# Two-layer GNN kernel: the first batch's sorted groups moved ahead of the first set's sort

## What is computed

```
h = relu(layernorm(x))
agg = segment_sum((h * node_vec1)[src], dst, 12500)      # layer 0: gather, sum by destination
x = x + agg * node_vec1_n2
h = relu(layernorm(x))
m = relu(h[src] + edge_attr_32)                          # layer 1: gather, add the edge's features
x = x + (1 + eps[0]) * h + segment_sum(m, dst, 12500)
```

## Time and profile before

| | us |
|---|---|
| median of three runs | 4798.12 (4794.34 to 4802.32) |
| the profiled execution | 4791.23 |
| its span | 4789.2 |
| busy in it: PE / DVE / ACT / POOL | 3721.2 / 3812.7 / 3261.3 / 3497.5 |

### The profile page before, as it was taken

How to read it: one execution, slowest core, us unless ns; L and a number is a source line. 1 busy time by engine, 2 the same in 40 slices (tenths; PEclk the granted TensorE clock), 3 DMA queues, 4 the chain that set the end, 5 groups by cost and what they waited for, 6 DMA issues and landing times.

```text
span 4789.2 us, 130194 instructions
## 1 busy us (share of the span) xinstructions
PE 3721.2 (78%) x43852; PEld 2888.9 (60%) x43852; DVE 3812.7 (80%) x11454; ACT 3261.3 (68%) x9090; POOL 3497.5 (73%) x3590
## 2 busy tenths in 40 slices
PE   0388888888888888888888899467767777777775
PEld 0266666666666666666666666356666666666664
DVE  9788888888888888888888886767777776777775
ACT  1377777777777777777777777456666766666664
POOL 6757777777777777777777777477777777777774
PEclk9999999999999999999999999778888888888887
DMA  6322222222222222222222221211212221211221
GB/s 111 63 51 54 57 54 54 54 56 54 54 54 56 54 53 54 56 54 53 54 56 54 53 54 44 72 39 54 57 43 54 57 57 54 58 49 48 57 57 26
DMA packets 439702, 262.77 MB, mean 55 GB/s; under 512 B 334660, under 2 KB 423732, under 8 KB 432632
## 3 DMA queue, kind: packets, MB, share of 16 engines
q1 hardware_dynamic: 322488, 187.55, 16.7%
q0 software_dynamic: 110816, 60.69, 6.7%
q10 hardware_dynamic: 5728, 5.82, 0.5%
HBM read 172.96 MB, written 80.85 MB: 53 GB/s over the span
## 4 chain that ended last, share of the span: by engine, by line
PE 32%; POOL 23%; DVE 19%; issue 13%; ACT 10%; DMA 2%; DVEq 1%; ACTq 0%; SPq 0%; POOLq 0%
POOL stage L759 22%; PE candidates L1247 18%; PE plain_ps L1259 7%; DVE arena L1753 7%; ACT message L987 5%; DVE arena L1729 4%; ACT centered L956 2%; PE sorted_agg L1187 2%; PE candidates L1157 1%; ACT arena L880 1%; POOL message L759 1%; PE key_rows L1230 1%; DMA stage<-in_edge_attr 1%; DVE counts L1475 1%; PE key_rows L1139 1%
## 5 line engine op out<-in xcount | busy, mean ns | idle before, releaser
L771 POOL DMA_INDIRECT records<-stage,place_i x1875 | 1879.0, 1002 | 696.2 <-issue 652.0
L759 POOL DMA_INDIRECT stage<-table,src_plain x1250 | 1246.9, 997 | 409.1 <-issue 377.3
L987 ACT ACTIVATE message<-candidates,member_is 128x96 bf16<-128x96 f32 x4560 | 1170.7, 377 | 429.4 <-PE candidates L1247 426.3
L1753 DVE TENSOR_SCALAR arena<-window_iota,dst_rel 128x224 bf16<-128x224 f16 (+1 forms) x4800 | 1091.2, 302 | 37.8
L880 ACT ACTIVATE arena<-key_rows 125x640 f16<-125x640 f16 x1000 | 653.2, 716 | 215.1 <-DVE arena L1729 83.2
L1187 PE MATMUL sorted_agg<-arena 128*96 128x224 bf16 (+1 forms) x5000 | 654.1, 285 | 161.0 <-DVE arena L1753 109.6
L1259 PE MATMUL plain_ps<-summed,message 128*96 128x224 bf16 x4560 | 609.2, 269 | 68.2 <-ACT message L987 68.2
L1187 PEld LDWEIGHTS sorted_agg<-arena 128*96 128x96 bf16 x5000 | 543.7, 137 | 186.1 <-issue 118.6
L1259 PEld LDWEIGHTS plain_ps<-summed,message 128*96 128x96 bf16 x4560 | 490.7, 128 | 269.6 <-ACT message L987 127.4
L1729 DVE TENSOR_SCALAR arena<-arena,row_key 125x1280 bf16<-125x1280 f16 x1000 | 554.7, 555 | 96.5 <-ACT arena L880 64.6
L1139 PE MATMUL key_rows<-ident,record 128*125 128x128 f16 x5000 | 425.8, 235 | 239.2 <-DMA record<-records 96.2
(11 more groups left out here) (228 smaller groups left out, 5139.0 us busy)
## 6 DMA issues: line engine op xcount, KB each, us to landing
record<-records SPq DMA_DIRECT2D x50, 1650.0 KB
stage<-in_edge_attr SPq DMA_DIRECT2D x125, 400.0 KB, 3.2
records<-pad SPq DMA_DIRECT2D x25, 1650.0 KB, 11.9
records<-stage,place_i POOLq DMA_INDIRECT x1875
stage<-table,src_plain POOLq DMA_INDIRECT x1250
message<-table,mid_src POOLq DMA_INDIRECT x288
xs<-in_x SPq DMA_DIRECT2D x8, 390.6 KB
table<-parts ACTq DMA_DIRECT2D x4, 585.9 KB
```

Source lines behind the costliest of these rows:

```text
L759: pool.indirect_dma_start(message[:, k, j, :] if l == 0 else rows[:, k, j, :], None, table0 if l == 0 else table1, bass.IndirectOffsetOnAx ...
L771: pool.indirect_dma_start(records, bass.IndirectOffsetOnAxis(ap=place_i[:, h, e:e + 1], axis=0), stage[:, h, e, :], None).then_inc(scatter ...
L987: last = nc.scalar.activation(direct_message[n % DB][:, m * WIDE:(m + 1) * WIDE], candidates[n % 2][:, m * WIDE:(m + 1) * WIDE], ACT.Copy, ...
L1753: last = nc.vector.tensor_scalar(dst_onehot(g, t), window_iota[:, 0:WA if tile == 0 else WT], dst_rel[:, h, tile:tile + 1], None, ALU.is_e ...
```

## The change

In batch 0 only, all three engines take the ten sorted groups first. DVE sorts the first set and reads the words of batch 0 behind them, right ahead of the wide steps. ACT issues the two DMAs of the trip behind the groups, and the direct keys of the first two wide steps are turned (PE) and copied (ACT) behind them as well.

```diff
@@ ACT, ahead of the layers
                     act.wait_ge(words_out, 32)
                     act.dma_start(set_left, words_rows[0:P, :]).then_inc(set_loaded, 16)
-                    act.wait_ge(set_steps, SET_STEPS)
-                    act.dma_start(ordered_rows[0:P, :], set_left).then_inc(words_out, 16)
-                    act.wait_ge(words_out, 48)
-                    act.dma_start(row_words, ordered_v[:, 0:SET, :]).then_inc(words_loaded, 16)
@@ ACT, step0
-                        if g in (7, 8) and not is_last(b):
+                        if g in (7, 8) and not is_first(b) and not is_last(b):
                             copy_direct_keys(b, g - 7)
...
                     over_main_groups(group)
+                    if is_first(b):
+                        act.wait_ge(set_steps, SET_STEPS)
+                        act.dma_start(ordered_rows[0:P, :], set_left).then_inc(words_out, 16)
+                        act.wait_ge(words_out, 48)
+                        act.dma_start(row_words, ordered_v[:, 0:SET, :]).then_inc(words_loaded, 16)
+                        copy_direct_keys(b, 0)
+                        copy_direct_keys(b, 1)
                     copy_sorted(b, 0)
@@ PE, step0
-                        if g in (7, 8) and not is_last(b):
+                        if g in (7, 8) and not is_first(b) and not is_last(b):
                             turn_direct_keys(b, h, g - 7)
...
                     over_main_groups(group)
+                    if is_first(b):
+                        turn_direct_keys(b, h, 0)
+                        turn_direct_keys(b, h, 1)
@@ DVE, ahead of the layers
-            dve.wait_ge(bounds_ready, 2 * PJ + 1)
-            sort_set(0, range(ROUNDS8))
-            dve.wait_ge(words_loaded, 16)
-            read_words(0, 0, 0)
@@ DVE, step0, behind over_main_groups(group)
                     else:
+                        if is_first(b):
+                            dve.wait_ge(bounds_ready, 2 * PJ + 1)
+                            sort_set(0, range(ROUNDS8))
+                            dve.wait_ge(words_loaded, 16)
+                            read_words(0, 0, 0)
```

## The result

The changed kernel takes 4812.59 us, the median of 18 runs (4806.34 to 4819.23). The kernel before, run beside it on the same chip, takes 4803.85 us, the median of 18 runs (4794.34 to 4813.91). The ratio is 1.0019, with a 95% interval of 1.0012 to 1.0026: some 9 us slower (5.8 to 12.5 us). The forecast was 9.0 us, and 4807 us in all. The measured time lies 5.6 us above that, as the kernel before does too: its median of 18 runs is 5.7 us above the 4798.12 us from which the forecast started. Two executions among the experiments, 7372.95 us of the kernel before and 6088.68 us of the one with all three steps, are far slower than the rest of their kernel and are left out of the ratios.

What follows compares the result with a forecast made beforehand. DVE was taken to set the time up to 304 us, with everything behind hanging on its end of batch 0. 7.2 + 0 + 0 + 1.5 + 0.3 = 9.0 us on 4798.1 gave 4807 us, range 4799 to 4816 us.

Steps and rivals of the forecast that it cites:

- The first hole: Ahead of DVE's first piece: waiting for record, turned and copied keys, including a second-group stall, costs 7.2 us (6.6 to 8).
- The groups: Batch 0's ten groups on DVE stay at 33.0 us; gain at most 1.6, loss beside transfers at most 3 us.
- Sort, trip and reading: On DVE after the groups: 38.5 us as before, change taken as 0, between -0.5 and +0.5 us.
- The new wait: Ahead of the wide steps DVE waits for direct keys turned and copied after the groups: 1.5 us (1.2 to 3).
- PE's restart: PE starts the wide steps slow after standing some 38 us; 0.3 us reaches DVE (0 to 1.8).
- Moved waits: Later sorted words and second-set load stay hidden by POOL's scatter, with 9 and 19 us to spare: 0 us.
- Rival A: The late start is made up within layer 0, so not slower: 4798 us; chance 0.17.
- Its own sign: Rival A's test: POOL's 28.8 us of standing before the scatter at 305.46 us shrinks without the scatter moving.
- Rival B: Groups suffer among transfers and PE's restart reaches DVE: 15.0 us slower, 4813 us; chance 0.13.
- the play between intervals: Argument for rival A: small waits in layer 0's loop; a different phase could be worth a few us either way.

Runs made afterwards that it cites:

- all three steps: Kernel before, with sorted words' trip beside the groups, first set stored first, batch 0's gathers after 50 of batch 1's scatters; ratio 0.9982, median 4786.31 us.
- the wait for keys alone: Kernel before in its old order, but DVE's first sort is held until the keys of the first two groups are copied; ratio 1.0019.
- quiet transfers: Changed kernel with the loads for batch 2 issued behind the second set's load; ratio 1.0028 against the kernel before.
- the plain delay: Kernel before with 40 chained small reductions on DVE ahead of batch 0's wide steps; ratio 1.0038.

## Why the prediction was right

The forecast was 4807 us, 9.0 us above the median of then; the ratio says 9.1 us (5.8 to 12.5). The number owes little to luck. The forecast is 9.0 us at DVE's end of batch 0. Counted from the request for record 0 the ranking of batch 2 ends 9.6 us later than before (means of two and three executions). From the start of the span it ends at 316.57 and 314.36 us, against 304.22, 305.08 and 306.51 before, 10.2 us later. By steps:

1. *The first hole, 7.2 us.* Counted from the same request it grew by 7.3 us, and the stall for the second group is 0.52 us, together 7.9 us, at the top of the range of 6.6 to 8. From the start of the span it was 8.4 and 8.3 us from the first MAX8 of before (153.43, 152.80) to the first one-hot (161.79, 161.12) in the two pairs of executions. From the request for the record to the first one-hot it is 9.7 and 10.2 us, where the prediction's 160.2 less 150.64 makes 9.6. The rest is that the request itself came at 150.64 to 152.09 us in these four executions. The chain of handoffs was sized well, with 0.1 to 0.6 us left out; that the wait for the first set and the record's request wander against each other was overlooked. The experiment with the wait for keys alone shows that a start this late is enough for the whole change.
2. *The groups, 33.0 us.* 34.7 and 33.5 us, against 33.0, 34.1 and 34.1 us before, and 35.3 without transfers. 0.52 us of each of the first two is the stall of step 1; without it the means are 33.6 and 33.7 us. Right, and the upper bound from transfers had no cause behind it.
3. *Sort, trip and reading, 38.5 us.* 38.9 us, from 196.53 to the end of the last comparison at 235.41 us, and 38.9 in the second execution; 38.5, 39.0 and 38.5 before. The trip's wait is 4.75 instead of 4.57 us. Right.
4. *The new wait, 1.5 us.* 1.68 us in both executions. Right in kind and size.
5. *PE's restart, 0.3 us.* The restart is there, larger than the rows before could show: 2.56 instead of 1.38 us for the six matmuls, and a granted clock of 0.50 from 238 to 241 us, the 1.2 GHz level, after the 37.69 us without work. From 245 us it reads 1.00, the 2.4 GHz level. The Trainium skill ("TensorE: Matmul & The Clock Gate", section "Part 1: The HAM clock gate") has the array at half rate after idleness, and here the granted clock agrees. But from the first wide one-hot to the ranking's end it takes 79.5 us (316.57 less 237.09), and 79.3 us before: it cost 0 to 0.2 us. In the earlier trace rows PE stood 0.91 us before the first products, so it had something to give. A lower clock elsewhere is not the cause either: the kernel that only waits for keys is as much slower, with a mean granted clock of 0.913 to 0.917 over its runs, where the kernel before has 0.912 to 0.918 beside it and the changed one 0.908 to 0.912.
6. *Moved waits, hidden.* The words were done at 235.4 us and the first gather began at 241.43. Hidden, with 6 us to spare instead of 9.

The bounds of these steps add up to more than the 7.3 to 12 us that the prediction gives for its own terms: the upper ends of steps 1, 3, 4 and 5 alone make 13.3 us. The measured sum needed neither end.

Rival A is refuted by the plain delay, which passed through layer 0 whole. Its own sign failed too: POOL stands 29.21 us before the next scatter, not less than the 28.84 before, and the scatter moved from 305.46 to 317.81 us. Rival B needed groups over 35 us or wide steps over 81. In the changed kernel's two executions they are 34.7 and 33.5 us, and 79.5 and 79.2, and quiet transfers did not make the groups faster. The prediction's doubt about A rested on the play between intervals; a shift of all batches is not play.

What stays open: the profiled executions of the changed kernel and of the one that waits for keys end 18 to 24 us behind the mean of the three of before (spans 4815.7, 4812.3 and 4818.3 against 4794.0 us), where the medians and ratios of all runs say 8 to 9. The last record of layer 0 is asked for at 2891.24 and 2891.12 us in the changed kernel and at 2872.80, 2874.08 and 2883.66 us in the kernel before, 7 to 18 us earlier. Within layer 0 executions of the same kernel wander as much: request by request, the second and third execution of before are within 2 us of each other at record 2 (404.84, 406.70) and 9.6 us apart at the last record of the layer (2874.08, 2883.66). I trust the 18 runs.

## What to carry to other kernels

Moving a full engine's work into its wait gains nothing when the moved work waits for a later input than the work that it displaces: compare when the inputs of both pieces are there before counting the hole as filled. Look for the second bound before promising a gain, by asking which engine waits less than a microsecond at the same place; here a delay at that place was paid in full, and an advance of 13 us needed the other chain moved too. With single profiled executions compare stretches between two marks of one run, not spans.

## What was not expected of the hardware

DVE goes through the same groups at one of two paces, and the program does not say which. From the third group on, each is two source one-hots and nine 128x224 destination one-hots on DVE. The starts of the nine in successive groups, from the second interval on, are 3.3 to 3.4 us apart in one profiled execution of the changed kernel and 3.15 to 3.2 us in the other. One such interval of each:

```profile
175.59 2.23 DVE L1755 TENSOR_SCALAR arena<-window_iota,dst_rel 128x224 bf16<-128x224 f16 x9
178.91 2.31 DVE L1755 TENSOR_SCALAR arena<-window_iota,dst_rel 128x224 bf16<-128x224 f16 x9
```

```profile
174.90 2.19 DVE L1755 TENSOR_SCALAR arena<-window_iota,dst_rel 128x224 bf16<-128x224 f16 x9
178.05 2.03 DVE L1755 TENSOR_SCALAR arena<-window_iota,dst_rel 128x224 bf16<-128x224 f16 x9
```

Over the ten groups that makes the 1.2 us between their two times. The kernel before has both paces too: its groups take 33.0 us in one execution and 34.1 in two. Transfers do not decide it, as the quiet kernel had the slow pace in most of these groups; the cause is open. And the store of all 25 batches' words was worth about 9 us of wait ahead of the first sort: with a set's share stored alone the load released DVE at 144.16 us instead of 153.43.
